# Softmax stage of a one-core hybrid layer: the weighted sums of two score steps made together

## The reference

```python
NUM_HEADS, HEAD_DIM = 16, 16
qkv = jnp.einsum('bsi,oi->bso', x, w_qkv)
q, k, v = jnp.split(qkv, 3, axis=-1)
q, k, v = (to_heads(q), to_heads(k), to_heads(v))
logits = jnp.einsum('bhsd,bhtd->bhst', q, k) * (1.0 / math.sqrt(HEAD_DIM))
mask = jnp.tril(jnp.ones((S, S), dtype=bool))
logits = jnp.where(mask, logits, neg_inf)
probs = jax.nn.softmax(logits, axis=-1)
probs = probs * mask.astype(probs.dtype)
out = jnp.einsum('bhst,bhtd->bhsd', probs, v)
out = out.transpose(0, 2, 1, 3).reshape(B, S, D_MODEL)
return jnp.einsum('bsi,oi->bso', out, w_out)

x = x + _L0_attn_b_ref(_layernorm(x, axis=-1), L0_attn_b_w_qkv, L0_attn_b_w_out)
```

## Time and profile before

| | |
|---|---|
| median of 3 runs | 10013.09 us (9991.96 to 10043.19) |
| profiled execution | 10030.08 us, its span 10027.0 us |
| mean granted TensorE clock | 0.79 of 2.4 GHz |
| busy in the span: PE, DVE, ACT, POOL | 76%, 54%, 34%, 17% |
| the step loop of one sequence, steps 0 to 47 | about 136 us of 626 us |

### The profile page before, as it was taken

The page is one execution under the profiler, slowest core; times in us unless marked ns, Lnnn a source line. Parts: engine busy times, 40 slices in busy tenths (PEclk is TensorE's granted clock), DMA queues, the critical chain, the costliest instruction groups (busy, mean ns, idle before and its releaser), DMA issues. The chain is left out here.

```text
span 10027.0 us, 116868 instructions
## 1 busy us (share of the span) xinstructions
PE 7586.4 (76%) x45086; PEld 4715.3 (47%) x45086; DVE 5453.0 (54%) x9637; ACT 3395.4 (34%) x6752; POOL 1707.5 (17%) x2232
## 2 busy tenths in 40 slices
PE   6777877778777787777877778777787776877768
PEld 4445454454544545445454454544545444454454
DVE  5456555455544555445565555554555555555555
ACT  2242422424224242242422424224242242423324
POOL 2103021020210302102021120210202112021120
PEclk8787877878778787787877878778787778877878
DMA  2110211102111021110211102111021110212102
GB/s 61 18 37 11 29 36 20 37 9 31 34 20 37 9 31 34 20 37 9 31 34 21 36 9 31 34 20 37 9 31 34 22 35 9 31 34 26 30 8 35
DMA packets 317627, 268.21 MB, mean 27 GB/s; under 512 B 205553, under 2 KB 243953, under 8 KB 316969
## 3 DMA queue, kind: packets, MB, share of 16 engines
q1 hardware_dynamic: 317020, 260.09, 15.4%
HBM read 48.74 MB, written 42.02 MB: 9 GB/s over the span
## 5 line engine op out<-in xcount | busy, mean ns | idle before, releaser
L1551 DVE TENSOR_REDUCE sa_nm<-ps 128x2 f32<-128x1024 f32 (+4 forms) x1280 | 1384.4, 1114 | 511.3 <-PE ps L1536 291.8
L1619 ACT ACTIVATE sa_pt<-ps 128x512 f32<-128x512 f32 (+3 forms) x3072 | 1284.5, 489 | 772.3 <-PE ps L1608 609.6
L1604 PE MATMUL ps<-sa_qs,sa_ks 99*128 99x512 bf16 (+3 forms) x3072 | 866.8, 338 | 38.9 <-ACT sa_pt L1619 34.8
L1532 PE MATMUL ps<-sa_ks,sa_qs 96*128 96x512 bf16 (+3 forms) x2560 | 710.6, 355 | 105.0 <-DMA sa_ks<-sa_parts 52.2
L1629 PE MATMUL ps<-sa_pt,sa_va 128*17 128x512 f32 (+3 forms) x6144 | 645.1, 494 | 0.0
L649 PE MATMUL ps<-rep,stack 128*32 128x512 f32 x4608 | 541.4, 631 | 128.4 <-PEq L387 128.4
L299 PE MATMUL ps<-ident,xn 128*128 128x128 f32 x1024 | 230.6, 419 | 504.5 <-PEq L318 237.2
L271 POOL TENSOR_TENSOR rstd<-vare,mhalf 128x2 f32<-128x2 f32 x256 | 178.2, 696 | 2427.8 <-DVE vare L263 2427.8
L1604 PEld LDWEIGHTS ps<-sa_qs,sa_ks 99*128 99x128 bf16 x3072 | 291.7, 99 | 617.7 <-ACT sa_pt L1619 424.2
L1198 PE MATMUL ps<-ident,mi_part 128*128 128x128 f32 x256 | 68.7, 435 | 551.5 <-DVE mi_part L1169 551.5
L280 ACT ACTIVATE xn<-x,shift,rstd 128x256 f32<-128x256 f32 x512 | 277.1, 592 | 554.3 <-POOL shift L273 547.7
(11 more groups left out here) (336 smaller groups left out, 15800.8 us busy)
## 6 DMA issues: line engine op xcount, KB each, us to landing
sa_qs<-sa_parts SPq DMA_DIRECT2D x384, 128.0 KB, 6.8
sa_ks<-sa_parts SPq DMA_DIRECT2D x384, 128.0 KB, 7.7
x<-in_x SPq DMA_DIRECT2D x17, 1024.0 KB, 5.6
rep<-paths SPq DMA_DIRECT2D x64, 256.0 KB, 4.4
bounce<-paths SPq DMA_DIRECT2D x32, 512.0 KB, 2.6
out_y<-x SPq DMA_DIRECT2D x16, 1024.0 KB, 5.4
rep<-paths SPq DMA_DIRECT2D x64, 255.8 KB, 5.4
rep<-paths SPq DMA_DIRECT2D x64, 255.5 KB, 6.5
```

The lines of the kernel that those rows point to most:

```text
L1532: last = nc.tensor.matmul(cols[:, i, :], qs[0:NCOMB * AD, g % NBUF, op.j + i, op.t * P:(op.t + 1) * P], ks[0:NCOMB * AD, g % NBUF, op.j + ...
L1551: nc.vector.tensor_reduce(nm[:, g % 2, op.c, op.t, op.j:op.j + op.heads], cols, AX.X, ALU.max, negate=True).then_inc(s.slot_free, 1)
L1604: last = nc.tensor.matmul(bank[:, off:], ks[0:QROWS, g % NBUF, j, kt * P:(kt + 1) * P], qs[0:QROWS, g % NBUF, j, n * BANK + off:(n + 1) * ...
L1619: nc.scalar.activation(pt[:, gs % 2, j, off:BANK], ring_bank(ring_use(gs, j))[:, off:], ACT.Exp, scale=RATIO).then_inc(s.ring_out, 1)
```

## The change

`SUM_STEPS = 2`: the sums of steps gs-2 and gs-1 are both made at the end of step gs, for even gs only; the last two steps' sums follow the loop. `pt` gets four step buffers in place of two (32 KB per partition instead of 16), and the exponential of step gs waits for the sums of step gs-4 in place of gs-2. To make room, `otm` is no longer a tensor of its own but the input buffer `x0`, which is not otherwise used in this stage. The instructions are the same in number and shape; only the order on PE and the wait of the exponentials differ.

```diff
 RING, RING_BANK, SUM_BANK = 3, 4, 7
+SUM_STEPS = 2
@@
-        otm = sb("sa_otm", [P, T, D])
+        otm = k.x0
@@
-        pt = sb("sa_pt", [P, 2, GH, BANK])
-        rest = pt[:].rearrange("p b j l -> p (b j) l")
+        pt = sb("sa_pt", [P, 2 * SUM_STEPS, GH, BANK])
+        rest = pt[:, 0:2].rearrange("p b j l -> p (b j) l")
@@ exp_act
-            if gs >= 2:
-                act.wait_ge(s.sums, gs - 1)
+            if gs >= 2 * SUM_STEPS:
+                act.wait_ge(s.sums, gs - 2 * SUM_STEPS + 1)
@@ exp_act and sums_pe
-                nc.scalar.activation(pt[:, gs % 2, j, off:BANK], ...
+                nc.scalar.activation(pt[:, gs % (2 * SUM_STEPS), j, off:BANK], ...
@@ the loop over steps on PE
-                    if gs:
-                        sums_pe(pe, gs - 1)
+                    if gs and gs % SUM_STEPS == 0:
+                        for before in range(gs - SUM_STEPS, gs):
+                            sums_pe(pe, before)
@@
-                sums_pe(pe, AG * NSTEPS - 1)
+                for before in range(AG * NSTEPS - SUM_STEPS, AG * NSTEPS):
+                    sums_pe(pe, before)
```

More of the change, by code:

```diff
@@ L1614, in exp_act @@
             off = max(0, kt * P - n * BANK)
-            if gs >= 2:
-                act.wait_ge(s.sums, gs - 1)
+            if gs >= 2 * SUM_STEPS:
+                act.wait_ge(s.sums, gs - 2 * SUM_STEPS + 1)
             for j in range(GH):
                 act.wait_ge(s.scores, gs * GH + j + 1)
-                nc.scalar.activation(pt[:, gs % 2, j, off:BANK], ring_bank(ring_use(gs, j))[:, off:], ACT.Exp,
+                nc.scalar.activation(pt[:, gs % (2 * SUM_STEPS), j, off:BANK], ring_bank(ring_use(gs, j))[:, off:], ACT.Exp,
                                      scale=RATIO).then_inc(s.ring_out, 1)
@@ L1629, in sums_pe @@
                 last = nc.tensor.matmul(ps[2 * AD * j:2 * AD * j + AD + 1, SUM_BANK, off:BANK], va[:, kt, g * GH + j, :],
-                                        pt[:, gs % 2, j, off:BANK], start=(kt == 0),
+                                        pt[:, gs % (2 * SUM_STEPS), j, off:BANK], start=(kt == 0),
                                         stop=(kt == (n + 1) * (BANK // P) - 1), skip_group_check=True)
```

## The result

The changed kernel took **10052.3 us** (median), the kernel before 10009.7 us in the same comparison: the ratio is 1.0035, with a 95% interval of 1.0021 to 1.0049. That is slower by 0.35%, and the median lies 1 us from the forecast. The forecast was right for the larger part of its reasons; one part, the clock outside the changed loop, was not in it, and took some experiments to see.

What follows compares the result with a forecast made beforehand. PE was taken to bound the kernel, DVE second. Terms summed to +2.4 us per sequence (4.4 saved, 6.8 of new waits and lost covers), x 16 = +38 us on the 10013 median: 10051 us, range 9985 to 10105.

Steps and rivals of the forecast that it cites:

- rival in which the slots take over: DVE, losing more per pair than laid out in steps 0 to 35, makes it about 10095 us; chance 0.20.
- waits of PE on DVE in steps 5 to 34: Sign expected in the profile: these waits go from nearly nothing to some 4 us.
- The price of a switch: Around each batch of sums on PE: 0.09 us in and 0.10 out, 0.19 in all; 23 batches fewer save 4.4 per sequence.
- joint of two batches: Between the two batches of a pair of sums: between 0.03 and 0.19 us, taken as 0.03.
- 9943 us: Rival of switching only: PE has no new waits and 70 us are gained; chance 0.07, with cases halfway.
- rival with a full switch at the joint: Joint within each pair costs a whole switch, so nothing is saved and the waits stay: 10122 us; chance 0.08.
- The ring: Steps 19/20, also 7/8 and 31/32: scores wait 0.27 + 0.21 us for banks, 0.19 saved: +0.29 per pair.
- The slot: Steps 17/18, also 5/6, 29/30: transpose waits 0.61 us for its slot, next maximum 0.20: +0.47 per pair.
- Steps 0 to 4: DVE bounds here and runs dry for 1.27 us, turn of step 4 comes 0.25 later: +0.71 us.
- Steps 13 to 16: With steps 25 to 28: nothing waits, four pairs at -0.19 us each, -0.76 in all.
- Steps 35/36: Sums of step 34 no longer fill PE's wait for POOL: +0.46 us, and +0.2 for the low clock.
- Steps 37 to 46: Scores follow ACT, but transposes and projection lie partly within ring waits: five pairs together -0.62 us.

Runs made afterwards that it cites:

- e4: Kernel before with the four buffers, sums paired only at steps 14, 26, 38, 40, 42 and 44; ratio 0.9951 to the kernel before.
- e3: Kernel before with the four buffers, sums paired only at steps 8, 20 and 32; ratio 1.0008 to the kernel before.
- e5: Kernel before with the four buffers, sums paired only at steps 6, 18, 30, transposes of steps 5, 17, 29 one step later; ratio 1.0006.
- e7: Changed kernel with the sums of step 34 back at the end of step 35, those of step 35 after step 36; ratio 0.9992 to the kernel before.
- e1: Changed kernel with one step's sums in every step again, as in the kernel before; only the buffer changes stay; ratio 0.9996 to the kernel before.
- e6: Kernel before with four buffers, sums paired only at steps 8, 20, 32, where the first maximum stands ahead of the scores; ratio 1.0002.
- e8: Changed kernel's buffers, order on PE from a searched table: 38 batches of sums, some mid-step, some maxima first; 9907.7 us, ratio 0.9890 to the kernel before.

## Why the prediction came out right, point by point

**The bound.** PE set the pace and still does; DVE's share of steps 0 to 35 fell from 78% to 76%, since they grew. The rival in which the slots take over, 10095 us, didn't come: DVE lost no more than laid out. One sign named for it came out smaller: waits of PE on DVE in steps 5 to 34 are 1.6 us in the view of waits, where some 4 had been named; the shorter ones don't show in that view.

**The price of a switch.** 0.09 in and 0.10 out were read right: e4's pairs give 0.21. The joint of two batches was taken as 0.03 and is nil (1.84 for two, where the terms of the forecast make it 1.86 with the joint in it). This is also the term that the page's rule bears on (the Trainium skill, "TensorEngine Tiling (Array Packing)", Key Properties): changing the mode drains the engine, changing the tile within it does not. The trace agrees in both halves. The rule says nothing of the buffers around PE, and by it alone the forecast would have been 9943 us, off by 1.1%. The rival with a full switch at the joint, 10122 us, is refuted by the same 1.84.

**The ring, +0.29.** 0.25 by measurement, and e3 shows that each pair brings it by itself. Its waits of 0.27 + 0.21 were measured as 0.31 + 0.20.

**The slot, +0.47.** 0.48. The wait of L1645 was forecast as 0.61 and is 0.54; the next maximum's as 0.20 and is 0.14. e5, which puts the sums back in front of the transpose, removes 0.38. Which buffer is to blame is thereby shown for the larger part of this term.

**Steps 0 to 4, +0.71.** 0.76 in steps 1 to 4. No experiment took this apart. The trace has new waits of PE for POOL ahead of the turns of steps 2 and 4 (0.27 and 0.52 us), so the turn named in the forecast does wait; how the 0.76 divide between it and DVE running dry is argued, not shown.

**Steps 13 to 16, 4 x -0.19.** The sum was right (-0.68 against -0.76), the division wasn't: -0.27 in the pair with the wide sums, -0.07 in the other. The rows at the turn of step 16 show why, before and after:

```profile
5518.26 0.63 PE L1629 MATMUL ps<-sa_pt,sa_va 128*17 128x256 f32 x8
5518.76 0.39 PE L1578 MATMUL ps<-identb,sa_mp 128*12 128x128 bf16 x4
...
5537.73 0.60 PE L1533 MATMUL ps<-sa_ks,sa_qs 96*128 96x512 bf16 x2
5538.25 0.39 PE L1579 MATMUL ps<-identb,sa_mp 128*12 128x128 bf16 x4
```

Before, the turn starts 0.50 us after the sums of 256 columns, where a score comes after 0.56 (5507.78 to 5508.34). After, it follows two maxima after 0.52 instead of their 0.44. So the turn has a way in of its own, which the sums ahead of it used to pay, and taking them away saves less than a whole switch. The forecast priced every removed batch the same.

**Steps 35/36, +0.46 and +0.2 for the clock.** +0.76 in the mean. The least value of the pair, in a sequence whose clock stays up, rose from 5.60 to 6.03: that is the lost cover, 0.43. The rest is clock, 0.3 where 0.2 was taken: 14 of 16 sequences have a stretch of about 3.4 us at 1.2 GHz there, and 11 before, and the sums now lie in it. e7 gives it back in the mean of this pair, but loses 0.38 of it again in steps 37/38; over the four steps it is 0.44 shorter than the changed kernel.

**Steps 37 to 46, -0.62.** -0.68.

**The total.** The loop's +35 us stands for the forecast's +38, and so does the ratio of 1.0035. The medians differ by 42.5, the profiled spans by 29. That the forecast's time is met to 1 us is luck: the runs show that work outside the loop can move the total by some 30 to 60 us either way, which is as much as the effect. The prediction had said that it would be wrong if any other stage changed its time; in the profile they did, but only by -6 us, and after and before have about the same time at the low level there (4086 and 4084). In e7 it would have failed on exactly that step: the expectation of 1.0027 held for the loop and missed the total by 0.35%. In e4 the same thing made a gain of 21 us look like 49.

## What to carry to other kernels

Grouping work on one engine to save its switching also groups its demand on the others: before counting the savings, ask for each buffer between them how long the engine now runs without the work that used to give the others time, and which wait that work was covering. Then group only where the trace shows no wait nearby: here six pairs chosen so took 1.2 us off a loop to which 23 pairs added 2.2, and a table that also moved single batches into the waits took off 6.8. And where the granted clock changes level within the stages, judge an edit by the length of its own loop over all passes, not by the total alone, and within the loop by the steps that are equally long in all of them.

## What the runs showed of the hardware that was not expected

- **The total moves with the clock of stages that nobody touched.** One stage of 650 matmuls took 95.5 us at a granted clock of 0.84 and 104.4 at 0.74, in the same execution. It moves from execution to execution of one kernel (10007.6 us at 0.797, 10075 at 0.790), from one time of running to another (the kernel before: 10015.8 and 10053.9 us), and it differs between kernels: e7 came out 0.3% faster, by its ratio, than its loop accounts for, and with a pause of 0.95 us per sequence 0.7% slower than the sum of its parts. The intervals of the ratios are 0.25% to 0.5% wide.
- **An idle time of PE can have a price beyond its length, but need not.** Behind the turn of step 36, with the order of before and 1.65 us idle, a stretch at 1.2 GHz followed in 11 of 16 sequences before, in 15 of e1, 3 of e6 and 1 of e3; with the order of e7 in 15 of 16, and in 1 of the same with the pause. After the 0.67 us of e8 it followed in none. So the idle time alone doesn't decide it, and what does is open.
- **Two batches in the same column groups join without cost**: 1.84 us for two of 0.98, less than the 0.03 that was allowed for it.
- **Waits hide in merged rows.** The view of waits gave less waiting on exponentials after (1.7 us) than before (2.3), although each ring pair had gained 0.5 of it; the row x3 of 1.12 us against 0.81 showed it.
